# Expert stage of a decoder: rows that carry a name, blocks that scatter their results

## The reference, cut to what matters

```python
def _moe(x, gate, expert_bias, w1, w2, w3, shared_w1, shared_w2, shared_w3):
    xt = x.reshape(-1, dim)                                  # 2048 tokens
    scores = sigmoid(xt @ gate.T)                            # 8 experts
    _, sel = top_k(scores + expert_bias[None, :], 2)
    top_scores = take_along_axis(scores, sel, axis=1)
    flat_sel = sel.reshape(-1)
    order = argsort(flat_sel, stable=True)
    token_idx, expert_ids = order // 2, flat_sel[order]
    routed = xt[token_idx] * top_scores.reshape(-1)[order][:, None]
    xb = routed.astype(bfloat16)
    for e in range(8):
        h = silu(xb @ w1[e].T) * (xb @ w3[e].T)              # 256 hidden
        out_r = out_r + where((expert_ids == e)[:, None], h @ w2[e].T, 0.0)
    hs = silu(xt @ shared_w1.T) * (xt @ shared_w3.T)
    out = (hs @ shared_w2.T).at[token_idx].add(out_r)
```

## Time and profile before

| | |
|---|---|
| median of 3 runs | 2942.64 us (2941.36 to 2946.05) |
| profiled execution, its time | 2947.47 us |
| its span, first to last instruction | 2945.7 us |
| mean granted clock of TensorE | 0.958 |
| busy: TensorE, VectorE, ScalarE, GpSimd | 90%, 68%, 50%, 41% of the span |
| experts phase, from its first transposes | 2674 us to the end, 272 us |
| its block loop, first to last expansion | 2796.2 to 2864.5 us |

### The profile page before, as it was taken

One profiled execution on the slowest core, in us unless ns is written; L12 is line 12 of the kernel. 1 busy time (PEld: TensorE's weight loads), 2 busy tenths in 40 slices (PEclk: granted clock), 3 DMA queues, 4 the chain that ended last, 5 costly groups with the idle time before them and its releaser, 6 DMA issues. The chain is left out here.

```text
span 2945.7 us, 47353 instructions
## 1 busy us (share of the span) xinstructions
PE 2639.9 (90%) x16941; PEld 1760.8 (60%) x16941; DVE 1988.5 (68%) x2542; ACT 1464.4 (50%) x2868; POOL 1199.9 (41%) x1106
## 2 busy tenths in 40 slices
PE   8999899888888888886999899999997889997886
PEld 5666645534444444443999777777775555556653
DVE  4788757689999999966112079999999733333353
ACT  3444413289999998862222166666666311112410
POOL 0000025446666565542222058688888500001304
PEclk9999999989999999997999999999999999997898
DMA  2123513269888887964002221011112271111163
GB/s 97 65 77 116 201 51 100 77 133 168 170 170 163 170 172 162 191 154 159 32 29 74 100 79 45 26 55 58 51 51 94 77 129 36 43 66 58 61 151 118
DMA packets 534873, 296.52 MB, mean 101 GB/s; under 512 B 438160, under 2 KB 482192, under 8 KB 530832
## 3 DMA queue, kind: packets, MB, share of 16 engines
q1 hardware_dynamic: 518720, 260.31, 35.1%
q0 software_dynamic: 15952, 33.56, 4.0%
HBM read 126.43 MB, written 62.78 MB: 64 GB/s over the span
## 5 line engine op out<-in xcount | busy, mean ns | idle before, releaser
L1181 DVE TENSOR_REDUCE xh_top<-xh_seen 128x1 f32<-128x512 f32 (+1 forms) x768 | 631.3, 863 | 46.0 <-PE xh_seen L1083 32.5
L1153 ACT ACTIVATE xh_prob<-xh_sc,xh_bias,xh_scale 128x1024 int16<-128x1024 f32 (+1 forms) x512 | 609.8, 1201 | 69.5 <-PE xh_sc L1083 69.3
L2328 POOL TENSOR_TENSOR ss_state<-ss_du,ss_b_all 128x1024 f32<-128x1024 f32 x128 | 445.7, 3495 | 169.4 <-PE ss_turned L1926 97.8
L1083 PE MATMUL xh_seen<-xh_kT,xh_qT 96*128 96x512 bf16 x1024 | 354.0, 387 | 81.8 <-DVE xh_top L1181 79.8
L2376 DVE TENSOR_TENSOR_SCAN ss_state<-ss_decay,ss_state 128x1024 f32<-128x1024 f32 x128 | 387.3, 3027 | 27.3 <-ACT ss_decay L2178 27.3
L1083 PE MATMUL xh_sc<-xh_kT,xh_qT 96*128 96x512 bf16 x1024 | 309.0, 384 | 1.3 <-ACT xh_prob L1153 1.3
L1207 POOL CAST xh_probT<-xh_pairs 128x2048 int16<-128x2048 uint8 x128 | 241.8, 1889 | 11.3 <-DMA xh_pairs<-xh_prob 2.7
L1083 PEld LDWEIGHTS xh_seen<-xh_kT,xh_qT 96*128 96x128 bf16 x1024 | 89.3, 97 | 242.8 <-DVE xh_top L1181 220.4
L1933 PE MATMUL ss_bank<-ss_xc,hold_w_conv 128*128 128x256 f32 x1024 | 229.3, 379 | 0.7 <-ACT ss_xc L2190 0.7
L2178 ACT ACTIVATE ss_decay<-ss_delta,ss_a 128x255 f32<-128x255 f32 x512 | 210.7, 496 | 0.4
L1933 PEld LDWEIGHTS ss_bank<-ss_xc,hold_w_conv 128*128 128x128 f32 x1024 | 190.0, 189 | 26.4 <-ACT ss_xc L2190 1.1
(11 more groups left out here) (392 smaller groups left out, 4886.5 us busy)
## 6 DMA issues: line engine op xcount, KB each, us to landing
ex_rows_in<-sa_zeros POOLq DMA_DIRECT2D x18, 1024.0 KB, 6.7
ss_b_all<-ss_states SPq DMA_DIRECT2D x8, 2048.0 KB, 7.2
xa_kT<-xp_kT SPq DMA_DIRECT2D x8, 768.0 KB, 5.3
xh_qT<-xa_qT SPq DMA_DIRECT2D x48, 128.0 KB, 3.2
xh_kT<-xa_kT SPq DMA_DIRECT2D x48, 128.0 KB, 3.3
ex_rows_out<-ex_oe SPq DMA_DIRECT2D x23, 256.0 KB, 2.2
sa_x<-in_x SPq DMA_DIRECT2D x8, 512.0 KB, 3.6
sa_y<-in_x SPq DMA_DIRECT2D x8, 512.0 KB, 10.9
```

What stands on the lines that cost most here:

```text
L1083: ins = pe.matmul(out[:, c * D:(c + 1) * D], qT[s][:, t * P:(t + 1) * P], kT[s][:, at + c * D:at + (c + 1) * D], start=True, stop=True)
L1153: act.activation(out, scores, ACT.Exp, bias=bias[t % RING][:, :], scale=scale[s][:, t:t + 1], accum_out=total[s][:, half, t:t + 1]).then_i ...
L1181: ins = v.tensor_reduce(top[t % RING][:, k:k + 1], scores[:, 0:n], AX.X, ALU.max)\
L2328: g.tensor_tensor(state[k % RING][:, :, :], du[s][:, :, :], spread(b_all[s][:, k, :], KD), ALU.mult)\
```

## The change

- A row of `ex_rows_in` becomes 544 bf16 numbers (`ROW`), 1,088 bytes. Numbers 512 and 513 hold a 32-bit name (`NAME`): the row of a new table `ex_results` into which the result of that row belongs, two rows for each token side by side. The scaled copies `xs` have the same width; GpSimd writes their names with an IOTA ahead of each tile's scatters. The pre-fill of the first phase writes names past the used part (2T + row) into the unused rows: an IOTA and a DMA in turn, each DMA waiting for the one before.
- SyncE loads for each block the names (`name`, a DMA of 256 pieces of 4 bytes) and then the transposed rows, into one of four buffers `rowT`. It stores no results any more.
- GpSimd scatters each block's result rows by their names, two indirect DMAs a block, while the blocks run. The gathers at the end are gone: SyncE loads each tile's results with one plain DMA of 512 KB, all eight behind the last scatter. The outputs are written in place of the results, so there are eight output buffers and no wait for a store.
- VectorE's plan leaves out `result_place` and packs the 23 expert numbers, eight to a 32-bit word; TensorE reads three words behind the last shared pass and takes each number out with a shift and a mask.
- The last `count_earlier` writes into a bank of `xin` and waits for `xT_sb` instead of `placed`. ScalarE's `scale(1)` and `front(3)` change places.

The core of the diff:

```diff
@@ self_attention @@
         def _(g):
-            g.memset(zeros[:, :], 0.0).then_inc(zeros_set, 1)
+            g.memset(unused[:, :, :], 0.0).then_inc(unused_set, 1)
...
                 for c in range(3 * n, min(3 * n + 3, chunks.shape[1])):
-                    g.dma_start(chunks[:, c, :], zeros[:, :]).then_inc(hold.zeroed, 16)
+                    g.wait_ge(unused_set, ONE + c + 1)
+                    if c > 0:
+                        g.wait_ge(hold.zeroed, 16 * c)
+                    g.iota(unused[:, :, D:D + 2].bitcast(mybir.dt.int32)[:, :, 0], [[1, UNUSED]],
+                           base=2 * T + c * UNUSED, channel_multiplier=EXPERT_ROWS // P).then_inc(unused_set, 1)
+                    g.wait_ge(unused_set, ONE + c + 2)
+                    g.dma_start(chunks[:, c, :], flat(unused[:, :, :])).then_inc(hold.zeroed, 16)
@@ experts, sync @@
             def load_rows(j):
...
-                if j >= 3:
-                    sp.wait_ge(up_ps, ONE + B + j - 2)
-                sp.dma_start_transpose(rowT[j % 3][:, :, :], rows_in[bass.ds(at, S), :]).then_inc(row_loaded[j % 3], 16)
-            for j in range(3):
+                if j >= 4:
+                    sp.wait_ge(up_ps, ONE + B + j - 3)
+                rows = rows_in[bass.ds(at, S), :]
+                sp.dma_start(name[:, j, :, :], rows[:, NAME].rearrange("(t p) o -> p t o", p=P),
+                             allow_slow_non_contiguous=True).then_inc(block_loaded[j % 4], 16)
+                sp.dma_start_transpose(rowT[j % 4][:, :, :], rows[:, 0:D]).then_inc(block_loaded[j % 4], 16)
+            for j in range(BLOCKS):
                 load_rows(j)
-            for j in range(BLOCKS):
-                if j + 3 < BLOCKS:
-                    load_rows(j + 3)
-                sp.wait_ge(oe_ready, ONE + j + 1)
-                sp.dma_start(block_rows(rows_out, j * S), oe[j % 3][:, :, :]).then_inc(oe_stored[j % 3], 16)
+            for i in range(3):
+                sp.wait_ge(oe_sent[i], 16 * TB * ((BLOCKS - 1 - i) // 3 + 1))
+            for n in range(B):
+                sp.dma_start(result[n], results[n * 2 * S:(n + 1) * 2 * S, :]
+                             .rearrange("(t p c) d -> p t (c d)", p=P, c=2)).then_inc(got[n], 16)
@@ experts, gpsimd @@
             for n in range(B):
+                if n >= 2:
+                    g.wait_ge(scattered[n % 2], 16 * 2 * TB * (n // 2))
+                g.iota(xs[n % 2][:, :, :, NAME].bitcast(I32)[:, :, :, 0], [[1, 2], [2 * P, TB]], base=2 * S * n,
+                       channel_multiplier=2).then_inc(named, 1)
+                g.wait_ge(named, ONE + n + 1)
                 g.wait_ge(placed, ONE + n + 1)
...
-            gather(0)
+            for j in range(BLOCKS):
+                g.wait_ge(block_loaded[j % 4], ONE + 32 * (j // 4 + 1))
+                g.wait_ge(oe_ready, ONE + j + 1)
+                for t in range(TB):
+                    g.indirect_dma_start(results, bass.IndirectOffsetOnAxis(ap=name[:, j, t, :].bitcast(U32), axis=0),
+                                         oe[j % 3][:, t, :], None).then_inc(oe_sent[j % 3], 16)
             for n in range(B):
-                if n + 1 < B:
-                    gather(n + 1)
                 inverse_root(g, ln, n)
@@ experts, tensor @@
                 pe.wait_ge(chosen, ONE + n + 1)
-                pe.wait_ge(placed, ONE + n)
+                if n < B - 1:
+                    pe.wait_ge(placed, ONE + n)
+                else:
+                    pe.wait_ge(xT_sb, ONE + B)
...
+            def load_experts():
+                pe.wait_ge(tab_ready, ONE + 1)
+                return [pe.value_load(experts_at[0:1, i:i + 1], min_val=0, max_val=E ** PER_WORD - 1) for i in range(WORDS)]
+            def expert(j):
+                return pe.snap((words[j // PER_WORD] >> (3 * (j % PER_WORD))) & (E - 1), min_val=0, max_val=E - 1)
...
-            e = expand_shared(B - 1, between=choose_experts)
+            expand_shared(B - 1)
+            words = load_experts()
@@ experts, scalar @@
             scale(0)
             odds(2)
+            front(3)
             scale(1)
-            front(3)
             odds(3)
@@ experts, vector: take and normal @@
                 if j >= 3:
-                    v.wait_ge(oe_stored[j % 3], ONE + 16 * (j // 3))
+                    v.wait_ge(oe_sent[j % 3], 16 * TB * (j // 3))
...
-                if n >= 2:
-                    v.wait_ge(stored[n % 2], ONE + 16 * (n // 2))
```

141 lines of the change are left out of this document (64 added, 77 removed).

## The result

| | before | after |
|---|---|---|
| median of six runs each, one chip | 2944.49 us (2941.36 to 2946.05) | 2928.03 us (2924.50 to 2933.78) |
| ratio | | 0.9948, 95% interval 0.9935 to 0.9961 |
| profiled execution, time | 2947.47 us | 2928.54 us |
| its span | 2945.7 us | 2926.3 us |

The gain is 16.5 us where 16.1 were forecast. The changed kernel was measured twice more for the experiments, word for word the same: on chip 8 it gained the same 16 us, on chip 3 nothing (2948.83 against 2947.22 us). So two things have to be explained: where the 16 us came from, and why they are not there on every chip.

A forecast was written before the change was run, and what follows sets the result against it. TensorE, busy nearly throughout, was taken as the bound, so gains had to be its idle stretches, low clock or the tail. 2.4 + 6.7 - 2.9 + 5.1 + 4.8 = 16.1 us off 2942.64 gave 2926.5, range 2920 to 2937.

The forecast's parts named there:

- First stage, 0: GpSimd's pre-fill of the row table, now chained DMAs and IOTAs: no effect, bounds minus 1 to plus 1 us.
- ScalarE's turn, 2.4: Routing in the experts stage: copying tile 3's transposed input first starts its routing 2.4 us earlier, bounds 2.0 and 2.54.
- The start of the loop, 6.7: Way into the block loop: two edits free TensorE, first rows become the gate, 6.7 us gained, bounds 6.0 to 7.3.
- The clock at the start, -2.9: Ahead of the block loop: TensorE idles 3 to 5 us and its lower clock costs 2.9 us, bounds 0 and 4.
- A block, 5.1: Block loop: loads leave earlier, 2.85 us a block instead of 3.106 over 20 blocks, 5.1 us gained, bounds 0 and 7.
- The covers: Block loop: SyncE's round 2.3 to 2.8 us, GpSimd's 2.53 and DMA's 2.26 have to fit in a 2.85 us block.
- the rival of the dear transpose: Block loop: wider rows make transposes dearer and DMA engines set the pace, 2931.6 or 2939.3 us; chance 0.18.
- The tail, 4.8: Last tiles: plain loads of results are hidden and VectorE alone sets the end, 4.8 us gained, bounds 3.5 and 6.
- one covers the other: Block loop: the rounds of SyncE, GpSimd and the DMA engines were taken to lie within a block's 2.85 us.
- The rival that put the danger at this place, the scatters: Block loop: GpSimd's scatters become the bound; gain gone at 1.83 us a scatter, 2953.5 us at 2.1; chance 0.06.
- The signs named beforehand: Block loop and tail: first expansion about 9 us earlier at clock 0.5, no row waits, starts 2.85 apart, results landed early.
- the signs of being wrong: Casts waiting for sent results, transposes over 5 us, first stage's inverse root behind the pre-fill, names costing SyncE a microsecond each.

The follow-up runs named there:

- ScalarE's turn alone: The kernel before with one edit, ScalarE copying tile 3's transposed input ahead of tile 1's four scaled copies: 2938.60 us against 2945.63 on chip 6, ratio 0.9981.
- the two kernels with four more semaphores: The changed kernel with five further edits, with 16 thrown-away products ahead of the loop (2930.29 us, chip 0) or with 4 (2926.28 us, chip 3).

## Why the prediction held, step by step

**First stage, 0.** Held. The inverse roots of the first stage stood 42.5 us apart before and stand so now; the cover that was reckoned as 18 us is 28.4, the idle time behind the third chunk's DMA. GpSimd is held for 14 us and not 24: the waits of the first two chunks are 6.2 and 3.9 us, and nothing waits for the third here:

```profile
145.39 0.13 POOL L389 IOTA sa_unused<- 128x8 int32 x1 [3.88 <-DMA ex_rows_in<-sa_unused]
145.84 0.55 POOL L392 DMA_DIRECT2D ex_rows_in<-sa_unused  x1 [0.32 <-POOL sa_unused L389]
174.79 0.72 POOL L82 TENSOR_TENSOR sa_rstd<-sa_shifted,sa_minus_half 128x2 f32<-128x2 f32 x1 [28.40 <-DVE sa_shifted L268]
```

**ScalarE's turn, 2.4.** Held: tile 3's routing starts 29.14 us behind the experts' start in place of 31.56.

**The start of the loop, 6.7.** Together with the turn 9.1 were forecast and 9.6 measured. The parts held too: IOTA and wait 0.44 for 0.5, the names' issue 0.52 for 0.45, and from the issue of the transposing load to the first matmul 3.46 for 3.3. What the sum gave to two edits belongs to one, the packing: beside it the counting pass's own bank is worth nothing, by the experiments above.

**The clock at the start, -2.9.** The mechanism held, the term was mis-sized. TensorE idled 8.3 us and not 3 to 5, in part because the second shared pass ran at 1.00 and not at 0.70 and because the three reads lie in that time; but the loss was 5.24 - 3.90 = 1.3 us over the first two expansions and 0.15 on the third. I had taken the loss of a pass of 10.1 us; the expansions at the lower clock were a shorter piece of work.

**A block, 5.1.** It takes 2.90 us where I took 2.85. That the term still came out larger, 5.7 us, has a reason that the sum missed: 3.106 was the mean of 22 periods with the quick first three among them, and the blocks behind these took 3.20. The loop as a whole gained 4.5 for the 2.2 of these two terms together: 1.5 of the surplus is the clock's, 0.6 the blocks', 0.2 lies behind the last expansion. Whether the blocks' gain is the fourth buffer's or that of the store that left SyncE's queue, no run shows. The covers held on this chip: SyncE's round 2.61 (2.3 to 2.8), GpSimd 0.96 + 0.30 twice, DMA 0.80 busy from 2797 to 2850 where 2.26 of 2.85 is 0.79. The profile's lines for the queues give, at 2.78 us a block, 1.53 us for transpose and names (1.43 reckoned) and 0.80 for the scatters (0.83). So the rival of the dear transpose fell: a transpose from rows 1,088 bytes apart costs the DMA engines 0.1 us more than a contiguous one if the names cost the 0.2 us estimated, and at most 0.3 (1.53 against 1.23) if they cost nothing. The Trainium skill, "DMA: Bandwidth & Descriptors", Latency and other measured facts, gives 261 GB/s for a transpose with a non-contiguous middle dimension and 350 to 400 for a contiguous one. That ratio didn't carry over to these transposes: by it they alone would take 1.65 to 1.9 us (an estimate), and 1.53 were measured with the names.

**The tail, 4.8.** 5.1 measured, and by its steps: the results landed hidden, TensorE waited for none, VectorE's 12.16 us for three tiles set the end. One small slip: ahead of tile 5's results the trace of before has waits of 0.49 and 0.24 us, not 0.49 and two like it.

**What was missed.** 1.1 us at the end of the program, behind the last store, which lands in 2.8 us as before. It is there in every kernel with the change, on every chip (10.8 to 10.9 us from the last output to the end of the span, 9.8 in before and in the kernel with ScalarE's turn alone), and 11.3 us in the two kernels with four more semaphores. I have no cause for it. And the loop's step "one covers the other" took the hand-over times between the engines, 0.03 to 0.3 us, for constants of the kernel. They aren't: on three of the four chips known by number those from TensorE grow to as much as 3 us, in the kernels where GpSimd issues scatters in the loop, and the whole gain goes. The rival that put the danger at this place, the scatters, had the right place, but its mechanism (a scatter of over 1.83 us) didn't occur; a scatter took 0.96 us everywhere. The time in that case, 2944 to 2949, lies outside the range that I gave.

**The signs named beforehand.** The first expansion came 9.6 us earlier, for about 9. The clock over it was 0.72, not 0.5. Two waits for rows are left in the loop, 1.6 us, where none was forecast. Of the signs of being wrong none showed.

**Luck.** The mechanisms held on the first chip and on chip 8, but that the number agrees to 0.4 us is in part luck. The terms brought 19.2 us in the profiles and not 16.1: 0.5 more at the start with the turn, 2.3 in the loop, 0.3 in the tail. The 1.1 us at the end and a profiled execution of before that stood 3.0 us above its median take it back to the 16.5 of the medians. And it was luck on which chip the change was measured: on chip 3 the same text gains nothing.

## To carry to other kernels

When a change moves transfers onto GpSimd's queue inside a tight loop between engines, measure it on several chips before believing the gain, and compare the stretches and not the totals: here, with the unchanged text of the changed kernel, two stretches stayed within 1 us on each chip while the third took 71 or 89. Once a gate has moved (here from TensorE to the arrival of rows), look at what idles in front of it: work that was ordered for the old gate, like the shared parts four tiles ahead, can now be ordered for the new one, and that was worth two thirds as much again as the change itself, some of it by a clock that stayed up.
